# A six-layer decoder block on one core: the delta rule's inverse is taken within 64-token halves, the squares are added on GpSimd, its inputs are made in one block, and x is loaded and stored in pieces

## The chip, the core and the metric

The kernel is one program on one core of one Trainium2 chip. The metric is the device time in microseconds (us) of the whole program; lower is better. Three runs of the kernel before took 6059.12, 6057.47 and 6052.54 us, median 6057.47. The core's engines run side by side, each through its own list of instructions in order: PE (TensorE, matrix products), DVE (VectorE), ACT (ScalarE), POOL (GpSimd) and SP (SyncE, which here only starts DMAs). They meet at semaphores: an instruction adds to one when it is done, another waits until it has reached a number. An engine whose next instruction waits does nothing else.

## The reference, cut to what matters

x has 4 batches of 512 tokens of 512 features. Six layers follow each other: a selective scan, a quantised linear layer, a mixture of experts, the delta rule, a cross attention and a ternary feed-forward layer. The change touches the ends of the first and the last, and the delta rule, for which the reference steps through the tokens, for each of 16 heads of 128 features:

```python
q, k, v = (silu(causal conv(h @ W)) for each);  q = l2norm(q) * K ** -0.5;  k = l2norm(k)
g = -exp(A_log) * softplus(h @ Wfa @ Wfb + dt_bias);   beta = sigmoid(h @ Wb)
def step(S, (qt, kt, vt, gt, bt)):
    S = S * exp(gt)[..., None]
    vd = (vt - S^T kt) * bt
    S = S + kt[:, None] * vd[None, :]
    return S, S^T qt
o = o * rsqrt(mean(o * o) + eps) * o_norm_w * sigmoid(h @ Wga @ Wgb);   x = x + o @ Wo
```

Here h is the layer norm of x. Within a chunk of 128 tokens the vd of a token depends on those before it through a strictly lower triangular matrix L of 128 x 128, so the kernel needs (I + L)^-1 for each chunk, head and batch.

## The kernel before, in words

All of x stays in on-chip memory (`main_x_rows`, 16 tiles of 128 tokens). `load_constants` loads it by one DMA of 4 MB and waits for it, and each layer runs as a block of its own that starts when the one before has ended on every engine. `store_result` stores x by one DMA after the last block.

The delta rule has three blocks. `layer_norm` takes the statistics of all 16 tiles, normalises each, and turns it on PE into hT. `low_rank` multiplies hT by wfa, wga and wb for each batch (`low_f`, `low_g`, `low_b`), then takes the products with wb a second time with tokens on the partitions (`low_col`, 64 products of 16 columns), from which ACT makes root_beta. hT, fgT and beta go to HBM. `delta_heads` is the third.

`delta_heads` works on 64 units, one for each head and batch. A unit has four chunks of 128 tokens, side by side in tiles of 128 x 512. The program is written out by hand as a pipeline: a unit passes through four stages, `front`, `middle`, `late` and `back`, one iteration apart, and in each of the 27 numbered slots of an iteration every engine does what the four stages have there, the oldest unit first. So while unit n is in `front`, unit n-2 is in `late` and unit n-3 in `back`. Slot numbers alone set the order on each engine.

- `front`, slots 0 to 11: products with the projection weights (`delta_rule_proj`, `delta_rule_level` at the v projection), convolutions and norms on DVE and ACT.
- `front`, slots 12 to 24: seven levels, for halves of 1, 2, 4, ... 64 tokens. A level goes POOL `suffix` (L1816), DVE `prefix` (L2059), DVE `qk_second` (L2001), POOL `k_first` (L1807), PE `delta_rule_level` (L2182), and `take` on DVE, two copies under a mask into QT and L (L1990). PE has two banks for the levels, so the product of one level waits until `take` has read the one two before.
- `late`, slots 13 to 21: POOL has solved the 16-token blocks (`solve`), SP has carried them through HBM into X, and the list `steps` extends the inverse to 128 tokens. With W = X and R = L W, the full inverse is (I - R + R^2 - ...) applied to W: nine products, each four times 128 x 128, and each read from one of two banks by ACT (copies WT, R, R2, R4T) or DVE (copies RT, R2T; three sums into X).
- `back`, slots 0 to 12: for the four chunks in turn v - S^T k, its product with X, the new state, and o. Then ACT squares o, and two products with a matrix of ones (slot 13) add the squares of q and of o over the features. ACT takes logarithm and exponential (slot 20), DVE gates (slot 26).
- slot 23: the product of four kept units with w_o (L2265), and slot 26 its sum into x.

Each entry of `steps` is (slot, result, left, right, who reads it, ACT copies and DVE reads of the unit that PE waits for).

## Time and profile before

| | |
|---|---|
| runs of the whole program | 6059.12, 6057.47, 6052.54 us; median 6057.47 |
| the profiled execution, first to last instruction | 6055.8 us |
| PE, DVE, ACT, POOL busy | 81%, 65%, 47%, 35% of it |
| the pipeline of 64 units, from its first DMA on | 1744 to about 4800 us |
| the two blocks ahead of it (norm, low rank) | 1640 to 1744 us |
| load of x, store of x | issued at 0.94 us, at 6042.91 us |

The profiled execution's span is 1.7 us below the median of the runs. It is the same program in one execution, seen by the profiler. The profile gives busy time, what released each wait, and the order of time on each engine. The share of busy time does not tell what bounds a stage of a pipeline; for that the order of time is read engine by engine.

### The profile page before, as it was taken

How to read it: one execution, taken by the hardware profiler on the slowest of the kernel's cores; microseconds unless marked ns; L12 is line 12 of the kernel's file. 1: busy time of each engine (PE TensorE's matmuls, PEld its weight loads, DVE VectorE, ACT ScalarE, POOL GpSimd, SP SyncE). 2: the span in 40 equal slices, each digit the busy share in tenths (PEclk: the TensorE clock that was granted, in tenths of full speed). 3: DMA queues.
4: the chain of work that ended last, by engine and by line, in shares of the span. 5: the costliest groups of instructions: out<-in, count | busy, mean ns of one | idle time of the engine just before them, and what ended most of it. 6: DMA issues, size and time to landing. Idle time of an engine off the chain costs nothing. (4 is left out here: it accounts for less than half of the span.)

```text
span 6055.8 us, 82551 instructions
## 1 busy us (share of the span) xinstructions
PE 4922.0 (81%) x24879; PEld 3229.1 (53%) x24965; DVE 3961.2 (65%) x6588; ACT 2819.8 (47%) x5024; POOL 2139.0 (35%) x2663
## 2 busy tenths in 40 slices
PE   5788747999577889988998899899898665888856
PEld 3556534566345666666666666666666432444423
DVE  4677664222337877877777777787777244888756
ACT  5555352111124555555555555555555213777632
POOL 2455400110215545445455454454454044000100
PEclk8899868999778999999999999999999787999989
DMA  2111005244331111111111111111110044111110
GB/s 61 29 29 29 15 28 194 73 144 157 122 99 50 37 48 42 43 55 50 43 40 49 55 47 44 49 40 41 52 46 28 11 136 140 54 54 54 42 57 28
DMA packets 355563, 365.99 MB, mean 60 GB/s; under 512 B 100193, under 2 KB 253281, under 8 KB 353921
## 3 DMA queue, kind: packets, MB, share of 16 engines
q1 hardware_dynamic: 335472, 286.73, 15.9%
q0 software_dynamic: 19744, 74.99, 3.5%
q8 instruction: 176, 2.88, 0.2%
q14 instruction: 171, 1.39, 0.1%
HBM read 264.76 MB, written 96.86 MB: 60 GB/s over the span
## 5 line engine op out<-in xcount | busy, mean ns | idle before, releaser
L1816 POOL TENSOR_TENSOR delta_rule_suffix<-delta_rule_suffix,delta_rule_prefix 128x256 f32<-128x256 f32 x448 | 513.6, 1146 | 1141.5 <-ACT delta_rule_prefix L1911 715.6
L2158 PE MATMUL delta_rule_proj<-delta_rule_hT,delta_rule_w_qkv 128*128 128x512 f32 x1024 | 466.4, 599 | 0.0
L2182 PEld LDWEIGHTS delta_rule_level<-delta_rule_qk_second,delta_rule_k_first 128*128 128x128 f32 x3072 | 392.9, 196 | 101.3 <-issue 86.6
L2182 PE MATMUL delta_rule_level<-delta_rule_qk_second,delta_rule_k_first 128*128 128x128 f32 x3072 | 425.6, 283 | 24.9 <-DVE delta_rule_L_large L1990 9.6
L481 DVE TENSOR_TENSOR_SCAN scan_hs<-scan_decay,scan_inp 128x512 f32<-128x512 f32 x256 | 308.6, 1216 | 194.4 <-PE scan_inp L543 90.9
L315 POOL TENSOR_TENSOR scan_hc<-scan_hs,scan_c_rows 128x512 f32<-128x512 f32 x256 | 334.6, 1312 | 282.1 <-DVE scan_hs L481 266.1
L2001 DVE TENSOR_TENSOR delta_rule_qk_second<-delta_rule_qk,delta_rule_prefix 128x512 f32<-128x512 f32 x448 | 363.0, 810 | 47.4 <-issue 12.1
L2059 DVE TENSOR_TENSOR delta_rule_prefix<-delta_rule_prefix 128x256 f32<-128x256 f32 x448 | 287.1, 641 | 160.2 <-PE delta_rule_level L2170 121.1
L1807 POOL TENSOR_TENSOR delta_rule_k_first<-delta_rule_qk,delta_rule_suffix 128x256 f32<-128x256 f32 x384 | 304.5, 793 | 196.3 <-PE delta_rule_level L2170 155.9
L2006 DVE SCALAR_TENSOR_TENSOR delta_rule_qk<-delta_rule_proj,delta_rule_conv_w,delta_rule_qk 128x511 f32<-128x511 f32 (+2 forms) x384 | 287.5, 749 | 103.7 <-ACT delta_rule_qk L1890 76.8
L2666 DVE TENSOR_REDUCE attend_top<-attend_scores 128x1 f32<-128x512 f32 x512 | 327.6, 682 | 42.3 <-DMA scan_c_rows<-bc_dram 42.3
L2700 ACT ACTIVATE attend_probs<-attend_scores,attend_top 128x512 f32<-128x512 f32 x512 | 345.6, 685 | 5.0 <-DVE attend_top L2666 5.0
L543 PEld LDWEIGHTS scan_inp<-scan_b_diag,scan_duT 128*128 128x128 f32 x2048 | 277.1, 199 | 112.1 <-issue 107.4
L553 PE MATMUL scan_y_ps<-scan_hc,main_ident 128*128 128x512 f32 x512 | 273.7, 617 | 66.5 <-POOL scan_hc L315 66.2
L1945 ACT ACTIVATE delta_rule_R<-delta_rule_inv 128x512 f32<-128x512 f32 x192 | 114.6, 597 | 425.2 <-PE delta_rule_inv L2217 425.2
L2158 PEld LDWEIGHTS delta_rule_proj<-delta_rule_hT,delta_rule_w_qkv 128*128 128x128 f32 x1024 | 185.5, 191 | 227.2 <-issue 186.1
L2626 PEld LDWEIGHTS attend_turned<-main_ident,attend_probs 128*128 128x128 f32 x2048 | 229.6, 141 | 110.9 <-ACT attend_probsT L2713 93.9
L543 PE MATMUL scan_inp<-scan_b_diag,scan_duT 128*128 128x128 f32 x2048 | 281.7, 283 | 2.7 <-ACT scan_duT L395 2.7
L2618 PE MATMUL attend_scores<-attend_k_stack,attend_q_stack 128*128 128x512 bf16 x449 | 163.8, 390 | 146.9 <-ACT attend_probs L2700 97.8
L2626 PE MATMUL attend_turned<-main_ident,attend_probs 128*128 128x128 f32 x2048 | 274.9, 278 | 2.6 <-ACT attend_probs L2700 1.6
L2684 DVE COPY attend_probsT<-attend_turned 128x512 f32<-128x512 f32 x256 | 177.1, 692 | 123.7 <-PE attend_turned L2626 108.8
L2265 PE MATMUL delta_rule_seq<-delta_rule_w_o,delta_rule_o_kept 128*128 128x512 f32 x512 | 234.6, 602 | 10.7 <-DMA delta_rule_w_o<-in_kda_wo 5.7
(466 smaller groups left out, 11678.2 us busy)
## 6 DMA issues: line engine op xcount, KB each, us to landing
parts_dram<-qkv_parts POOLq DMA_DIRECT2D x64, 512.0 KB, 10.5
moe_w_d<-in_w_down SPq DMA_DIRECT2D x39, 512.0 KB, 4.3
scan_c_rows<-bc_dram SPq DMA_DIRECT2D x64, 256.0 KB, 3.7
delta_rule_w_qkv<-in_kda_wq SPq DMA_DIRECT2D x64, 256.0 KB
delta_rule_w_qkv<-in_kda_wk SPq DMA_DIRECT2D x64, 256.0 KB
delta_rule_w_qkv<-in_kda_wv SPq DMA_DIRECT2D x64, 256.0 KB
delta_rule_inv_beta<-beta_dram SPq DMA_DIRECT2D x64, 256.0 KB
delta_rule_w_o<-in_kda_wo SPq DMA_DIRECT2D x64, 256.0 KB, 4.7
```

The costliest lines, as they stand in the source:

```text
L315: pool.tensor_tensor(hc[:, u % RING, :], hs[:, u % RING, :], c_rows[:, n, :], ALU.mult).then_inc(weighed, 1)
L481: dve.tensor_tensor_scan(hs[:, u % RING, :], decay[:, u % RING, :], flat(inp_ps[u % INPUTS]), 0.0, ALU.mult, ALU.add).then_inc(scanned, 1)
L543: last = pe.matmul(inp_ps[u % INPUTS][:, c, :], duT[:, b % 2, c, k * P:(k + 1) * P], b_diag[:, n, c, :], start=True, stop=True)
L1807: pool.tensor_tensor(halves(k_first[:, i % 2, :], s, 0), halves(qk[p][:, 1, :], s, 0), first, ALU.mult).then_inc(k_ready, 1)
L1816: pool.tensor_tensor(first, first, whole_second, ALU.mult).then_inc(suffix_done, 1)
L2001: dve.tensor_tensor(qk_second[:, i % 2, :, :].rearrange("p j (n s) -> p j n s", s=s), qk[p][:].rearrange("p j (n two s) -> p j n two s", t ...
L2006: return dve.scalar_tensor_tensor(to[:, back_by:S], src[:, 0:S - back_by], conv_w[i][:, h, TAPS - 1 - back_by:TAPS - back_by], to[:, back_ ...
L2158: last = pe.matmul(to, w_qkv[p][:, i, k, :], hT[:, b % 2, k, :], start=(k == 0), stop=(k == DT - 1))
L2182: last = pe.matmul(level_ps[(i + 1) % 2][:, c, :], left, qk_second[:, i % 2, :, c * CHUNK // 2:(c + 1) * CHUNK // 2], start=True, stop=True)
L2626: last = pe.transpose(turned[i % 2][:, q, :], probs[:, j % 2, q, i * P:(i + 1) * P], g["ident"][:])
L2666: dve.tensor_reduce(top[:, j % 2, i:i + 1], scores[i][:], AX, ALU.max, negate=True).then_inc(max_done, 1)
L2700: act.activation(probs[:, j % 2, i, :], scores[i][:], ACT.Exp, bias=top[:, j % 2, i:i + 1], accum_out=head_sums[:, j % 2, i:i + 1]).then_i ...
```

## The change

1. x is loaded by four DMAs of 1 MB; nothing waits in `load_constants`, and the scan waits for batch b where it first reads it. x is stored tile by tile (256 KB) in the last block, as each tile is finished.
2. `layer_norm` and `low_rank` become one block, `delta_inputs`. The statistics are taken for the first 4 tiles, then for the other 12; a batch's low-rank products follow its turning; the four batches' products with wb (padded to 32 columns) go to four groups of 32 partitions of one bank; `low_col` is replaced by four transposes of exp(-b).
3. The inverse series stops within 64-token halves: R2 and R4T and the last sum go. The corner below the diagonal of the 128 x 128 inverse is made of 64 x 64 products: the first half's inverse turned (slot 21), times the corner of L (slot 23), times the second half's inverse (slot 25), and ACT copies each.
4. `take` of the last level copies its 64 x 64 corners without a mask, into QT and `L_top`.
5. POOL adds the squares of q to those of o in slot 17, and one product with ones in slot 19 takes the place of the two in slot 13.
6. SP returns the solved blocks of the first unit of a pair, waits for them and loads X, before it stores those of the second.

```diff
-                sp.dma_start(g["x"][:], g["x_dram"].rearrange("(t p) d -> p t d", p=P)).then_inc(x_loaded, 16)
-                sp.wait_ge(x_loaded, 16)
+                load_rows(sp, g, 0)
@@ scan, SP after dtproj
+                for b in range(1, B):
+                    load_rows(sp, g, b)
@@ scan, DVE, chores(b, 0)
+                        dve.wait_ge(g["x_loaded"][b], 16)
@@ last block, SP
+                    for t in range(NT):
+                        sp.wait_ge(out_added, t + 2)
+                        sp.dma_start(g["out_dram"][t * P:(t + 1) * P, :], g["x"][:, t, :]).then_inc(x_stored, 16)
+                    sp.wait_ge(x_stored, 16 * NT)
@@ delta_inputs, DVE
+                statistics(0)
+                invert(0)
+                for t in range(TPB):
+                    normalize(t)
+                statistics(1)
+                invert(1)
@@ delta_inputs, PE
+                def betas():
+                    for k in range(DT):
+                        for b in range(B):
+                            last = pe.matmul(b_ps[b * PAD:(b + 1) * PAD, :], wb[:, k, :], hT[:, k, b * S:(b + 1) * S],
+                                             start=(k == 0), stop=(k == DT - 1))
+                    last.then_inc(b_done, 1)
...
+                for t in range(TPB):
+                    turn(t)
+                pe.wait_ge(w_loaded, 32)
+                for b in range(1, B):
+                    for t in range(b * TPB, (b + 1) * TPB):
+                        turn(t)
+                    low_rank(b - 1)
+                betas()
+                low_rank(B - 1)
+                pe.wait_ge(b_exp, 1)
+                for i in range(TPB):
+                    last = pe.transpose(col_ps[:, i, :], beta[:, i * P:(i + 1) * P], g["ident"][:])
@@ delta_heads, slots and steps
-        SQUARE_SLOT, NORM_SLOT, LN_SLOT, EXP_SLOT, GATED_SLOT, OUT_SLOT, ADD_SLOT = 12, 13, 20, 20, 26, 23, 26
+        SQUARE_SLOT, SUM_SLOT, NORM_SLOT, LN_SLOT, EXP_SLOT, GATED_SLOT, OUT_SLOT, ADD_SLOT = 12, 17, 19, 20, 20, 26, 23, 26
...
                  (17, "W", "RT", "W", SUB, 2, 1),
-                 (17, "R2", "RT", "R", COPY_A, 2, 1),
-                 (17, "R2T", "R", "RT", COPY_V, 2, 2),
-                 (19, "W", "R2T", "W", ADD, 3, 3),
-                 (19, "R4T", "R2", "R2T", COPY_A, 3, 3),
-                 (21, "W", "R4T", "W", ADD, 4, 4)]
+                 (17, "R2T", "R", "RT", COPY_V, 2, 1),
+                 (19, "W", "R2T", "W", ADD, 2, 3),
+                 (21, TURN_FIRST, None, None, COPY_A, 2, 4),
+                 (23, CORNER_T, None, None, COPY_A, 3, 4),
+                 (25, CORNER, None, None, COPY_A, 4, 4)]
@@ SP, return_blocks
                     for p in range(2):
                         for c, to in enumerate(diagonal(g["solved_dram"][p])):
-                            sp.dma_start(to, block_rows(solved, p, c)).then_inc(solved_stored, 16)
-                    sp.wait_ge(solved_stored, 16 * 2 * CHUNKS * (m + 1))
-                    for p in range(2):
+                            sp.dma_start(to, block_rows(solved, p, c)).then_inc(solved_stored[p], 16)
+                        sp.wait_ge(solved_stored[p], 16 * CHUNKS * (m + 1))
@@ POOL, back
+                    if slot == SUM_SLOT:
+                        pool.wait_ge(o_squared, n + 1)
+                        pool.tensor_tensor(o_square[:], o_square[:], q_square[:, n % 4, :], ALU.add).then_inc(o_summed, 1)
@@ DVE, take
+                        if i == NL - 1:
+                            reach(dve, inv_done, NS * (n - 2) + 8)
+                            data = level_ps[(i + 1) % 2][:].rearrange("p c (j m) -> p c j m", j=2)
+                            dve.tensor_copy(QT[n % 3][FIRST, :, SECOND], data[FIRST, :, 0, :])
+                            dve.tensor_copy(L_top[p][:], data[FIRST, :, 1, :]).then_inc(level_read, 1)
+                            return
@@ PE, late
+                                if name == TURN_FIRST:
+                                    last = pe.transpose(inv_ps[i % 2][FIRST, c, FIRST], X[p][FIRST, c, FIRST], g["ident"][FIRST, FIRST])
+                                elif name == CORNER_T:
+                                    last = pe.matmul(inv_ps[i % 2][SECOND, c, FIRST], L_top[p][:, c, :], first_T[:, c, :], start=True, stop=True)
+                                elif name == CORNER:
+                                    last = pe.matmul(inv_ps[i % 2][FIRST, c, FIRST], corner_T[:, c, :], X[p][SECOND, c, SECOND],
+                                                     start=True, stop=True)
@@ PE, back
-                        pe.wait_ge(o_squared, n + 1)
+                        pe.wait_ge(o_summed, n + 1)
                         pe.wait_ge(state_done, (CHUNKS - 1) * (n + 1))
-                        pe.matmul(flat(seq_ps), g["ones"][:], q_square[:, n % 4, :], start=True, stop=False)
-                        pe.matmul(flat(seq_ps), g["ones"][:], o_square[:], start=False, stop=True).then_inc(o_norm_done, 1)
+                        pe.matmul(flat(seq_ps), g["ones"][:], o_square[:], start=True, stop=True).then_inc(o_norm_done, 1)
```

The first place is PE from slot 16 to the start of the next iteration, with buffer numbers (`inv0`, `level1`); a row is line, operation, what is written and read, and shape. Before:

```order
L2182 MATMUL delta_rule_level1<-delta_rule_qk_second,delta_rule_k_first 128x128 x4
L2217 MATMUL delta_rule_inv1<-delta_rule_X1,delta_rule_RT 128x128 x4
L2217 MATMUL delta_rule_inv0<-delta_rule_R,delta_rule_RT 128x128 x4
L2217 MATMUL delta_rule_inv1<-delta_rule_RT,delta_rule_R 128x128 x4
L2206 MATMUL delta_rule_proj1<-delta_rule_fgT,delta_rule_w_g 128x512
L2182 MATMUL delta_rule_level0<-delta_rule_qk_second,delta_rule_k_first 128x128 x4
L2217 MATMUL delta_rule_inv0<-delta_rule_X1,delta_rule_R2T 128x128 x4
L2217 MATMUL delta_rule_inv1<-delta_rule_R2T,delta_rule_R2 128x128 x4
L2182 MATMUL delta_rule_level1<-delta_rule_qk_second,delta_rule_k_first 128x128 x4
L2217 MATMUL delta_rule_inv0<-delta_rule_X1,delta_rule_R 128x128 x4
L2182 MATMUL delta_rule_level0<-delta_rule_qk_second,delta_rule_k_first 128x128 x4
L2265 MATMUL delta_rule_seq<-delta_rule_w_o,delta_rule_o_kept 128x512 x4
```

The same stretch of PE after the change, from R2T on:

```order
L2342 MATMUL delta_rule_inv0<-delta_rule_RT,delta_rule_R 128x128 x4
L2324 MATMUL delta_rule_proj1<-delta_rule_fgT,delta_rule_w_g 128x512
L2300 MATMUL delta_rule_level0<-delta_rule_qk_second,delta_rule_k_first 128x128 x4
L2377 MATMUL delta_rule_seq<-delta_rule_o_square,main_ones 128x512
L2342 MATMUL delta_rule_inv1<-delta_rule_X1,delta_rule_R2T 128x128 x4
L2300 MATMUL delta_rule_level1<-delta_rule_qk_second,delta_rule_k_first 128x128 x4
L2333 MATMUL delta_rule_inv0<-main_ident,delta_rule_X1 64x64 x4
L2300 MATMUL delta_rule_level0<-delta_rule_qk_second,delta_rule_k_first 128x128 x4
L2389 MATMUL delta_rule_seq<-delta_rule_w_o,delta_rule_o_kept 128x512 x4
L2335 MATMUL delta_rule_inv1<-delta_rule_RT,delta_rule_L_top1 64x64 x4
L2300 MATMUL delta_rule_level1<-delta_rule_qk_second,delta_rule_k_first 128x128 x4
L2337 MATMUL delta_rule_inv0<-delta_rule_X1,delta_rule_WT 64x64 x4
```

R2T goes to the other bank, the norm's product stands behind the fourth level, and two of the three small products stand behind the product with w_o. Between the first level and the next unit's projections there are three steps of four 128 x 128 products and one 128 x 512 product fewer, and three steps of four 64 x 64 ones more.

The second place is POOL in slots 14 to 18, before:

```order
L1807 TENSOR_TENSOR delta_rule_k_first<-delta_rule_qk,delta_rule_suffix 128x128x2
L1816 TENSOR_TENSOR delta_rule_suffix<-delta_rule_suffix,delta_rule_prefix 128x128x2
L1807 TENSOR_TENSOR delta_rule_k_first<-delta_rule_qk,delta_rule_suffix 128x64x4
L1816 TENSOR_TENSOR delta_rule_suffix<-delta_rule_suffix,delta_rule_prefix 128x64x4
L1807 TENSOR_TENSOR delta_rule_k_first<-delta_rule_qk,delta_rule_suffix 128x32x8
```

and after the change:

```order
L1915 TENSOR_TENSOR delta_rule_suffix<-delta_rule_suffix,delta_rule_prefix 128x128x2
L1906 TENSOR_TENSOR delta_rule_k_first<-delta_rule_qk,delta_rule_suffix 128x64x4
L1915 TENSOR_TENSOR delta_rule_suffix<-delta_rule_suffix,delta_rule_prefix 128x64x4
L1971 TENSOR_TENSOR delta_rule_o_square<-delta_rule_o_square,delta_rule_q_square 128x512
L1906 TENSOR_TENSOR delta_rule_k_first<-delta_rule_qk,delta_rule_suffix 128x32x8
```

The sum of the squares stands ahead of the fourth level's `k_first`. In both the slots of the levels are unchanged.

## Rows read from the trace of the kernel before

**Rows 1.** Order of time, first 30 us: start, length, engine, line, operation, idle before.

```profile
1.70 0.23 DVE L65 CAST main_ident<-main_ident 128x128 bf16<-128x128 f32 x1 [1.70 <-POOL main_ident L59]
...
19.81 2.46 DVE L438 BATCH_NORM_STATS2 scan_stats<-main_x_rows 128x6 f32<-128x512 f32 x4
```

**Rows 2.** DMA issues: destination, source, count, KB each, us to landing.

```profile
small_dram<-delta_rule_L_small SPq DMA_DIRECT2D x64, 256.0 KB, 2.0
...
main_x_rows<-in_x_dram SPq DMA_DIRECT2D x1, 4096.0 KB, 14.2
...
out_dram<-main_x_rows SPq DMA_DIRECT2D x1, 4096.0 KB, 12.5
...
fg_dram<-low_fgT SPq DMA_DIRECT2D x4, 512.0 KB, 3.1
```

**Rows 3.** Order of time, the last 16 us.

```profile
6041.26 0.75 DVE L2997 SCALAR_TENSOR_TENSOR main_x_rows<-ternary_ffn_out_ps,ternary_ffn_scales,main_x_rows 128x512 f32<-128x512 f32 x1 [6.43 <-PE ternary_ffn_out_ps L3027]
6042.91 0.39 SPq L74 DMA_DIRECT2D out_dram<-main_x_rows  x1
```

**Rows 4.** Order of time, norm and low rank, up to the pipeline's first DMA.

```profile
1640.19 9.59 DVE L101 BATCH_NORM_STATS2 norm_kda_stats<-main_x_rows  x16 [4.35 <-PEq L3119]
...
1652.33 1.01 DVE L113 TENSOR_SCALAR norm_kda_h<-main_x_rows,norm_kda_mean_var,norm_kda_rstd 128x512 f32 x2 [0.50 <-issue]
...
1687.39 3.60 PE L1440 MATMUL low_g<-kda_in_hT,low_wga 128*128 128x512 f32 x8
...
1715.66 24.35 PE L1445 MATMUL low_col<-low_wb,kda_in_hT 128*128 128x16 f32 x128
...
1744.24 0.41 SPq L1694 DMA_DIRECT2D delta_rule_conv_w<-in_conv_q_w  x1
```

**Rows 5.** Order of time, PE in the cross attention: products into four partition groups.

```profile
5121.13 1.06 PE L2638 MATMUL attend_out_ps<-attend_probsT,attend_v_head 128*32 128x512 f32 x8
```

**Rows 6.** A stretch: us, busy (count) of PE, PEld, DVE, ACT, POOL, granted clock, DMA.

```profile
1830.00:4650.00 2820.00, 2512.29 (x13286) 1771.07 (x13286) 2220.14 (x3676) 1497.64 (x2322) 1428.73 (x1853) 0.98 0.16 46
```

**Rows 7.** Order of time, PE, one unit's late slots, and the next unit's first product.

```profile
3023.04 1.13 PE L2217 MATMUL delta_rule_inv<-delta_rule_RT,delta_rule_R 128*128 128x128 f32 x8 [0.99 <-DVE delta_rule_X L2093]
...
3029.66 1.13 PE L2182 MATMUL delta_rule_level<-delta_rule_qk_second,delta_rule_k_first 128*128 128x128 f32 x8
3030.62 3.60 PE L2265 MATMUL delta_rule_seq<-delta_rule_w_o,delta_rule_o_kept 128*128 128x512 f32 x8
...
3034.95 0.60 PE L2192 MATMUL delta_rule_proj<-main_ident,delta_rule_k_square 128*128 128x128 f32 x4
...
3057.49 1.92 PE L2170 MATMUL delta_rule_level<-delta_rule_qk 128*128 128x128 f32 x8
```

**Rows 8.** Order of time, DVE, late slots of the same unit and of the next.

```profile
3015.99 0.99 DVE L2059 TENSOR_TENSOR delta_rule_prefix<-delta_rule_prefix 128x256 f32<-128x256 f32 x1
...
3019.95 0.42 DVE L2059 TENSOR_TENSOR delta_rule_prefix<-delta_rule_prefix 128x256 f32<-128x256 f32 x1
...
3022.16 0.73 DVE L2093 TENSOR_TENSOR delta_rule_X<-delta_rule_X,delta_rule_inv 128x512 f32<-128x512 f32 x1
3024.20 0.69 DVE L2091 COPY delta_rule_R2T<-delta_rule_inv 128x512 f32<-128x512 f32 x1 [1.31 <-PE delta_rule_inv L2217]
...
3029.09 0.43 DVE L1990 COPY_PREDICATED delta_rule_L_small<-delta_rule_level_mask,delta_rule_level 128x256 f32<-128x256 uint16 x1
```

**Rows 9.** Order of time, DVE, the next unit's copy of RT.

```profile
3065.85 0.69 DVE L2091 COPY delta_rule_RT<-delta_rule_inv 128x512 f32<-128x512 f32 x1 [0.78 <-PE delta_rule_inv L2217]
```

**Rows 10.** Order of time, POOL in the first of the two units.

```profile
3015.97 0.73 POOL L1807 TENSOR_TENSOR delta_rule_k_first<-delta_rule_qk,delta_rule_suffix 128x256 f32<-128x256 f32 x1
...
3017.12 1.23 POOL L1816 TENSOR_TENSOR delta_rule_suffix<-delta_rule_suffix,delta_rule_prefix 128x256 f32<-128x256 f32 x1 [0.43 <-DVE delta_rule_prefix L2059]
...
3032.13 1.27 POOL L1820 TENSOR_TENSOR delta_rule_k_square<-delta_rule_qk,delta_rule_suffix 128x512 f32<-128x512 f32 x1
```

**Rows 11.** What ended PEld's idle time before line 2215, 1830 to 4650: us, times.

```profile
  DMA delta_rule_X<-solved_dram: 17.7, 7
```

223 lines of the change are left out of this document (148 added, 75 removed).

## Prediction

> **What bounds the kernel now.** I read the ends of the program first, then the blocks ahead of the pipeline, then one unit of the pipeline engine by engine.
>
> At the start the whole 4 MB of x is waited for. It is issued at 0.94 us and lands 14.2 us later, at 15.1, while the other work of that block ends at 1.93 [rows 1, 2]. At the end the last sum into x is done at 42.01 (all times of that stretch are 6000 and more), the store starts at 42.91 and lands 12.5 us later, at 55.4 [rows 2, 3]. Both transfers stand alone on the path.
>
> The norm and low rank blocks take from 1640.19 to 1744.24, 104.0 us. The reader is to see that the engines work one after the other there: DVE takes all statistics for 9.6 us before anything is normalised, the products with wb run again as `low_col` for 24.35 us, and nothing of the pipeline starts before [rows 4].
>
> The pipeline is PE at first sight: 2512 of 2820 us busy, 89% [rows 6]. But the order of time of one unit shows two different halves. Of the level and inverse slots (about 3012.7 to 3035) the reader is to see that PE starts the level product at 3029.66 just 0.14 us after DVE ended the `take` that frees its bank (3029.09 + 0.43) [rows 7, 8]. DVE has been at work there with hardly a gap: its one long wait is 1.31 us for R2T, whose product PE itself held back 0.99 us because its bank still waited for DVE's sum into X [rows 7, 8]. So up to that level DVE's chain sets the pace, and PE's own work counts only behind it. From 3034.95 on the order is that of the projections and of the four chunks, which the change leaves as it is. The period is therefore read at 3034.95, the first product of the next iteration.
>
> **The start.** The block now ends at 1.93 plus the 0.5 us that lay between landing and the next block (15.1 to 15.6 before); everything behind moves by 15.1 - 1.93 = 13.2 us. x's first reader was at 19.81 and will be at about 6.6. The first 1 MB, issued at 0.94, must be there: between 2.0 us (256 KB) and 14.2 us (4 MB) [rows 2], by proportion 4.4, so it lands at 5.4. The other 3 MB are wanted much later. Parameter loads queue behind it and may lose 1 to 2 us. **Take 13; bounds 8 to 13.2.**
>
> **The end.** The last 256 KB are issued at about 42.1 and land 2.0 us later if like the 256 KB stores of the pipeline, at 44.1, and the 0.9 + 0.4 us of block end and program end remain: 45.4 for 55.8. **Take 10.4; bounds 0 (12.5 us whatever the size) and 10.4.** The other 15 stores lie beside the last layer's work.
>
> **The inputs.** Statistics of 4 tiles are 4 x 0.60 = 2.4 us (9.59 / 16); before, 2.5 us lay between the last statistic and the first normalised tile (1649.8 to 1652.33), for 4 tiles some 1.7. First tile at 1644.3, the four done at 1646.4 (0.5 each). Twelve more statistics take 7.2, and 2.3 for the root: 1655.9. The next four tiles are turned in 3 us: 1659. From there PE has work without a gap: four batches of two products of 3.60 are 28.8, eight tiles turned at 0.6, the time of four transposes [rows 7], 4.8, the wb products, and four transposes, 0.6 [rows 4]. The wb products now go to four partition groups. In the attention, eight such passes of 512 columns end within 1.06 us, where eight passes on the full width take 3.60 [rows 4, 5]: four times as fast. So 32 passes are 4 x 1.0 = 4.0, and 14.4 if the overlap failed. That gives 1697.2; PE's clock starts low, 2 us; then DVE's sum and two copies (2 us) and SP's store of fgT, 0.5 + 3.1 [rows 2]: about 1706 for 1744.2. **Take 38; bounds 27 and 41.** `low_col` is 24.35 of it, the rest is statistics and turning laid beside products.
>
> **One unit of the pipeline, normal clock.** Removed from PE: three steps of eight passes (0.9 each) and one product of 0.86; added: three steps of eight, eight and four short passes. On DVE one sum into X goes, behind the level that decides.
> - What the DVE chain gains. R2T goes to the other bank and no longer waits for the sum. DVE ends that sum at 3022.89 (3022.16 + 0.73), and would copy R2T at once instead of at 3024.20: 1.3 earlier.
> - What POOL's sum costs it. It starts when `suffix` of the third level ends, 3018.35, and takes 1.27 like the other 128 x 512 product [rows 10]; `k_first` follows, 3019.7 to 3020.5. DVE wants `prefix` at 3019.95. Beside a `k_first` (3015.97 + 0.73 = 3016.70) the same operation did not take 0.42 but 0.99 and ended at 3016.98, 0.28 behind it [rows 8, 10]. So it ends at 3020.8 instead of 3020.4: 0.4 later. Bounds: 0 and 1.3, the whole sum.
> - So `take` and the level product behind it come 0.9 earlier, 3028.8.
> - Behind it on PE: 5.29 us to 3034.95 as before, with the w_o product in it [rows 7], and now two short steps, CORNER_T and CORNER; the turning falls in a gap. No row shows a 64 x 64 product. A full pass is 0.11 of 128 columns, half the columns are 0.055, 0.45 a step; a 16-column pass is 0.19 at half clock (24.35 / 128, with full weight loads [rows 4]), 0.095 at full, 0.76 a step. I take 0.55, nearer to the columns, since here the weights are half as many too. Two steps: 1.1; bounds 0.9 and 1.8 (a full step each).
> - Sum: -0.9 + 1.1 = **+0.2 us a unit; bounds -0.4 and +0.9.** The moved norm product (slot 19) ends long before the logarithm is wanted for the w_o product; PE has room for it, since DVE decides.
>
> The Trainium skill, TensorEngine Tiling (Array Packing), section Tiling Modes, says that changing the tiling mode drains TensorE. This kernel would change it four times a unit on the path. By the attention's row, with its eight passes over in 1.06 us and its mode changed twice around them, that is next to nothing; by the page, a tail of some 0.2 us four times would make it 0.8 a unit more, 50 us: 6026, which is the second rival's case.
>
> **One unit with a clock dip.** Granted clock 0.98 over 2820 us means 2820 x 0.02 / 0.5 = 113 us at 1.2 GHz instead of 2.4 [rows 6]. At 3057.49, behind the chunks' products with their gaps, the eight passes take 1.92 instead of 1.13 and the next eight are slow too, some 3.3 us: about 34 dips, one in two units [rows 7]. In such a unit PE comes late, and DVE waits 0.78 for RT [rows 9]. The two norm products that lay ahead of it are gone, so this 0.78 is gained. Mean: +0.2 - 0.39 = -0.2 a unit, for 62 of the 64 units (the first and the last run partly alone) **-12 us; bounds -50 and +45.**
>
> **X.** PE waits seven times for X, 17.7 us in all [rows 11]. The first X of a pair is now asked for four stores earlier, 1.5 to 2 us each time, but PE also wants it earlier. **Take -8; bounds 0 and -14.**
>
> The wait of a unit's first chunk for the corner's copy has 4 us of projections ahead of it. SP's added wait stands before stores that nobody wants for one more unit. Both cost nothing.
>
> **Sum.** 6055.8 - 13 - 10.4 - 38 - 12 - 8 = 5974.4 in the profiled execution, which stands 1.7 below the median of the runs: **5976 us.**
>
> **Rivals.**
> - *PE sets the period after all.* Then a unit loses 3 x 0.9 + 0.86 - 0.45 - 2 x 0.55 = 2.0 us, 124 us instead of 12: 5864. For it: 89% busy, and that PE's removed work is large. Against it: the 0.14 us between `take` and the level product. 0.18, with half of it a mixture near 5920 (POOL's sum costs DVE nothing, short passes are cheap).
> - *The short products are dear* (drains, weight loads that nothing covers): 0.7 a unit more, 43 us: 6019. For it: no row has their price. Against it: the attention's row. 0.20.
> - *The clock, on the other side.* PE has gaps of about 1 us more in the level slots, where it waits for DVE. If the granted clock falls there too, in every unit, 3.3 us at 1.2 GHz lose 1.65 behind the deciding level, and the dip behind the chunks in every unit another 0.4: 2.05 x 62 = 127 us: 6103, slower. It decides from 82 / 62 = 1.3 us a unit. For it: dips follow stretches with gaps. Against it: PE stays over 80% busy in these slots, and I see dips only behind the chunks. 0.07. The Trainium skill, SBUF — State Buffer, section SBUF: two separate sides, has another way to lose: the port that VectorE and GpSimd share is locked by one for a whole instruction. By that rule POOL's sum could block DVE for 1.27 us a unit; the rows show 0.28 behind a shorter one, and the sum would be 54 us more, not enough alone.
> - *The change is not as told in the inputs* (products with wb not side by side): 10 us, inside the range.
>
> **How the numbers follow.** Forecast (DVE decides, the period stays within 0.5 us) 0.55, own range 5945 to 6010; PE's rival 0.18; dear products 0.20; clock 0.07. The measurement tells no change from one of 0.2%, 12 us. The three block terms give 61 us, and only the clock, or dear products at their worst together with a lost end, eats them: faster 0.90, same 0.03, slower 0.07. The range 5915 to 6035 leaves out the lower half of PE's rival (0.09) and most of the clock's.
>
> **What would show it.** The scan's first statistics at about 6.6 us; the last store landing within 3 us; `delta_inputs` 65 to 68 us long, with the 32 wb passes in about 4. In the pipeline: a period within 0.5 us of the one before; the level product ahead of the w_o product still within 0.2 us of the `take` that frees its bank; R2T's copy right behind the sum into X; the short steps 0.4 to 0.6 us each. A period shorter by over 1 us refutes the claim that DVE decides; one longer by as much says that the short products or the clock are dearer than taken.

## The result, and the profile after

The changed kernel takes 5991.01 us (median of 4 runs, 5984.97 to 5995.06) where the kernel before took 6055.66 in the runs beside it: a ratio of 0.9897, 95% interval 0.9884 to 0.991. The forecast was 5976, in a range of 5915 to 6035. The profiled execution spans 5993.5 us, 62.3 less than before. Between the places named by the rows ahead of the prediction, that difference is made up like this (gain in us, what was predicted in brackets):

| | | |
|---|---|---|
| up to the first statistics of the norm ahead of the pipeline | 1640.19 to 1627.17 | 13.0 (13) |
| from there to the pipeline's first DMA | 104.05 to 61.50 | 42.5 (38) |
| pipeline, from there to the next norm's statistics | 3071.16 to 3071.64 | -0.5 (20: 12 and 8 for X) |
| from there to the last sum into x | 1225.86 to 1229.44 | -3.6 (0) |
| from the last sum to the end | 14.54 to 3.75 | 10.8 (10.4) |

So the three block terms came, and the pipeline's 20 us did not. The 3.6 us lost behind it are spread over the blocks there, in which only the stores of x are new; 1.6 of them lie in the cross attention. That block has the same instructions throughout, and took 629.3 to 631.7 us in eleven of the fourteen profiled executions of this document and 638.5 to 638.6 in three. So a difference of this size is no sign of an effect. First the ends, in order of time (start, length, engine, line, operation, idle before and what ended it):

```profile
3.64 0.43 SPq L276 DMA_DIRECT2D scan_d_skip<-in_d_skip  x1
...
7.62 0.88 DVE L419 TENSOR_SCALAR scan_d_diag<-main_ident,scan_d_skip 128x128 f32<-128x128 f32 x4 [5.30 <-DMA scan_d_skip<-in_d_skip]
...
8.51 1.28 DVE L435 BATCH_NORM_STATS2 scan_stats<-main_x_rows 128x6 f32<-128x512 f32 x2
...
5989.75 0.75 DVE L3126 SCALAR_TENSOR_TENSOR main_x_rows<-ternary_ffn_out_ps,ternary_ffn_scales,main_x_rows 128x512 f32<-128x512 f32 x1 [6.17 <-PE ternary_ffn_out_ps L3156]
5990.52 0.33 SPq L3086 DMA_DIRECT2D out_dram<-main_x_rows  x1
```

The scan's first statistics start at 8.51 where they started at 19.81 [rows 1]; 6.6 was expected. The small load of d_skip, issued at 3.64, lands only at about 7.6. It takes 4.0 us where it took 1.7 in the kernel before: now the first 1 MB of x stands ahead of it in SP's queue. That is the 1 to 2 us that the prediction set aside for it. At the end 3.0 us are left behind the last sum, where there were 13.8 [rows 3].

The block of inputs, against [rows 4]:

```profile
1627.17 2.47 DVE L1454 BATCH_NORM_STATS2 kda_in_stats<-main_x_rows 128x6 f32<-128x512 f32 x4 [4.28 <-PEq L3249]
...
1632.72 7.21 DVE L1454 BATCH_NORM_STATS2 kda_in_stats<-main_x_rows 128x6 f32<-128x512 f32 x12
...
1671.80 3.64 PE L1550 MATMUL kda_in_b<-kda_in_hT,kda_in_wb 128*32 128x512 f32 x32
...
1682.34 0.60 PE L1565 MATMUL kda_in_col<-main_ident,kda_in_beta 128*128 128x128 f32 x4
...
1688.67 0.40 SPq L1794 DMA_DIRECT2D delta_rule_conv_w<-in_conv_q_w  x1
```

The 32 passes into four partition groups take 3.64 us, as the attention's row had it [rows 5]; four transposes replace the 24.35 us of `low_col`.

Now one unit of the pipeline at the normal clock, PE from the unit's first level to the next iteration's first product, against [rows 7]:

```profile
2997.51 1.06 PE L2288 MATMUL delta_rule_level<-delta_rule_qk 128*128 128x128 f32 x8
...
3001.23 1.13 PE L2300 MATMUL delta_rule_level<-delta_rule_qk_second,delta_rule_k_first 128*128 128x128 f32 x8 [1.33 <-DVE delta_rule_QT L2182]
...
3008.89 1.02 PE L2377 MATMUL delta_rule_seq<-delta_rule_o_square,main_ones 128*128 128x512 f32 x2
3009.76 1.05 PE L2342 MATMUL delta_rule_inv<-delta_rule_X,delta_rule_R2T 128*128 128x128 f32 x8
3011.01 1.13 PE L2300 MATMUL delta_rule_level<-delta_rule_qk_second,delta_rule_k_first 128*128 128x128 f32 x8 [0.20 <-DVE delta_rule_L_small L2108]
3012.07 0.41 PE L2333 MATMUL delta_rule_inv<-main_ident,delta_rule_X 64*64 64x64 f32 x4
3013.65 1.13 PE L2300 MATMUL delta_rule_level<-delta_rule_qk_second,delta_rule_k_first 128*128 128x128 f32 x8 [1.16 <-DVE delta_rule_L_small L2108]
3014.61 3.60 PE L2389 MATMUL delta_rule_seq<-delta_rule_w_o,delta_rule_o_kept 128*128 128x512 f32 x8
3018.14 0.68 PE L2335 MATMUL delta_rule_inv<-delta_rule_RT,delta_rule_L_top 64*64 64x64 f32 x8
3018.75 1.16 PE L2300 MATMUL delta_rule_level<-delta_rule_qk_second,delta_rule_k_first 128*128 128x128 f32 x8
3019.84 0.67 PE L2337 MATMUL delta_rule_inv<-delta_rule_X,delta_rule_WT 64*64 64x64 f32 x8
```

and DVE in the same unit, against [rows 8]:

```profile
3004.97 0.81 DVE L2177 TENSOR_TENSOR delta_rule_prefix<-delta_rule_prefix 128x256 f32<-128x256 f32 x1
...
3007.59 0.71 DVE L2211 TENSOR_TENSOR delta_rule_X<-delta_rule_X,delta_rule_inv 128x512 f32<-128x512 f32 x1
3008.22 0.67 DVE L2209 COPY delta_rule_R2T<-delta_rule_inv 128x512 f32<-128x512 f32 x1
...
3010.44 0.42 DVE L2108 COPY_PREDICATED delta_rule_L_small<-delta_rule_level_mask,delta_rule_level 128x256 f32<-128x256 uint16 x1
3010.85 0.69 DVE L2211 TENSOR_TENSOR delta_rule_X<-delta_rule_X,delta_rule_inv 128x512 f32<-128x512 f32 x1
...
3013.08 0.42 DVE L2108 COPY_PREDICATED delta_rule_L_small<-delta_rule_level_mask,delta_rule_level 128x256 f32<-128x256 uint16 x1
```

The reader is to see three things. The level product ahead of w_o (3013.65) starts 0.15 us behind the `take` (3013.50), as forecast, and R2T's copy stands right behind the sum into X. A short step occupies 0.61 us (3018.14 to 18.75) and the full step behind it 1.09 (3018.75 to 19.84) for 0.89 elsewhere. And DVE's last sum into X (3010.85) starts just as PE ends the product for it, 3009.76 and 0.89 and some 0.15 to be seen: 3010.8. The two engines arrive there together, which no row of before showed so plainly, and which the prediction did not weigh.

### The profile page after: what moved, and what is told of

Read it like the earlier page. It is cut to its first block and busy times, and to the rows that moved or that the text cites. A ratio compares the mean times of both kernels' runs of the same rounds, so it can differ in the third digit from the quotient of the medians.

```text
span 5993.5 us, 81416 instructions
## 1 busy us (share of the span) xinstructions
PE 4792.9 (80%) x24371; PEld 3098.5 (52%) x24457; DVE 3930.6 (66%) x6523; ACT 2807.4 (47%) x5085; POOL 2208.3 (37%) x2728
## 5 line engine op out<-in xcount | busy, mean ns | idle before, releaser
L2300 PE MATMUL delta_rule_level<-delta_rule_qk_second,delta_rule_k_first 128*128 128x128 f32 x3072 | 444.8, 289 | 174.4 <-DVE delta_rule_L_small L2108 105.3
L2177 DVE TENSOR_TENSOR delta_rule_prefix<-delta_rule_prefix 128x256 f32<-128x256 f32 x448 | 326.5, 729 | 171.1 <-PE delta_rule_level L2288 125.9
L2790 DVE TENSOR_REDUCE attend_top<-attend_scores 128x1 f32<-128x512 f32 x512 | 327.7, 682 | 42.5 <-DMA delta_rule_inv_beta<-beta_dram 42.5
L2730 POOL COPY attend_v_head<-xattn_v_tiles 128x64 f32 x128 | 24.5, 236 | 586.7 <-PE attend_out_ps L2762 586.3
```

The source lines that it names most:

```text
L2177: dve.tensor_tensor(halves(prefix[:], HALVES[i], 1), halves(prefix[:], HALVES[i], 1), whole_first, ALU.mult).then_inc(prefix_done, 1)
L2300: last = pe.matmul(level_ps[(i + 1) % 2][:, c, :], left, qk_second[:, i % 2, :, c * CHUNK // 2:(c + 1) * CHUNK // 2], start=True, stop=True)
L2790: dve.tensor_reduce(top[:, j % 2, i:i + 1], scores[i][:], AX, ALU.max, negate=True).then_inc(max_done, 1)
```

## The experiments

All changes are against the kernel after, where not said otherwise. "Period" is the distance between two units' first product of the next iteration (the place 3020.44 above) where the clock is normal; "slow" counts the units, of the 59 periods that follow the fifth start, that are 0.3 to 1.9 us longer. Some are longer still and not in that count: 3 before, 5 after, 11 in e_old_pipeline, 9 in e_squares_early, at most 6 elsewhere. Ratios are to the kernel before, with 95% intervals.

| | median us | ratio | period | slow |
|---|---|---|---|---|
| before | 6055.66 | 1 | 45.06 | 21 |
| after | 5991.01 | 0.9897 (0.9884 to 0.991) | 45.38 | 24 |
| e_old_pipeline | 6005.77 | 0.9914 (0.9901 to 0.9926) | 45.06 | 22 |
| e_sum_only | 6077.43 | 1.003 (1.002 to 1.004) | 46.08 | 38 |
| e_squares_early | 6018.82 | 0.9939 (0.9926 to 0.9953) | 45.12 | 26 |
| e_squares_pe | 6083.27 | 1.0051 (1.0038 to 1.0064) | 46.20 | 43 |
| e_copies_act | 5991.46 | 0.9891 (0.9876 to 0.9905) | 45.35 | 26 |
| e_norm_late | 5917.74 | 0.9771 (0.9759 to 0.9784) | 44.49 | 16 |
| e_corner_early | 5953.10 | 0.9824 (0.9808 to 0.984) | 44.64 | 24 |
| e_corner_double | 6083.68 | 1.0044 (1.0031 to 1.0056) | 46.31 | 50 |
| e_batch_late | 5984.51 | 0.9877 (0.9862 to 0.9891) | 45.38 | 26 |
| e_stores_first | 5998.78 | 0.9903 (0.9888 to 0.9918) | 45.38 | 21 |
| v_combined | 5871.24 | 0.9693 (0.968 to 0.9705) | 43.80 | 26 |
| v_squares_early | 5872.74 | 0.9692 (0.9679 to 0.9705) | 43.80 | 20 |

**e_old_pipeline**: the kernel before with parts 1 and 2 of the change alone.

> The kernel before with only the new ends (loads and stores of x in pieces) and the new block of inputs; the 64 units run as before. Theory 1 (by the traces: the pipeline's block lasted 3071.2 us before and 3071.6 after, so its change is worth nothing): 5990 us, as the kernel after within 6, ratio to before 0.989. Theory 2 (the pipeline gained its predicted 20 us and the three block terms gave less than the traces seem to say): 6011 us, ratio 0.993.

Measured 6005.8, between the two. Its profile runs the pipeline's old instructions at the old period of 45.06, and yet its pipeline, from the first DMA to the next norm's statistics, takes 3087.6 us where that of the kernel before took 3071.2. Of these 16 us, 11 lie in the 61 periods from the third start on (2811.8 for 2800.7): there are 22 slow units for 21, but 11 periods that are longer still for 3. So one profiled execution tells the pipeline's total no better than some 16 us. The pipeline's part of the change is worth about 15 us by the medians, 10 by the ratios (whose intervals overlap), 16 against this trace (3071.6 for 3087.6) and nothing against the trace of the kernel before. None of these is shown to be the right one. In the 61 periods alone the kernel after takes 2810.4 us, 1.4 less than this run and 9.7 more than the kernel before; the rest of each difference lies where the pipeline fills and empties.

**e_squares_pe**: back to two products, in slot 19, no sum on POOL.

```diff
...
-                        pe.wait_ge(o_summed, n + 1)
+                        pe.wait_ge(o_squared, n + 1)
...
-                        pe.matmul(flat(seq_ps), g["ones"][:], o_square[:], start=True, stop=True).then_inc(o_norm_done, 1)
+                        pe.matmul(flat(seq_ps), g["ones"][:], q_square[:, n % 4, :], start=True, stop=False)
+                        pe.matmul(flat(seq_ps), g["ones"][:], o_square[:], start=False, stop=True).then_inc(o_norm_done, 1)
```

> The kernel after, but the squares are not added on POOL: PE takes both products with the matrix of ones, in slot 19. Theory 1 (DVE's chain decides up to the level ahead of the w_o product, and POOL's sum holds up one prefix by 0.38 us a unit, while PE waits 1.17 us there and has room for 0.43 us more): period 45.0 for 45.38 us, 62 units, 24 us less: 5967 us, ratio 0.9855. Theory 2 (PE's work sets the pace): 0.43 us more a unit, 6018 us, ratio 0.994. Theory 3 (POOL's sum costs DVE nothing): 5991.

It went the other way: 92 us slower. Here my expectation also had a wrong price. One such product is 0.86 us, not 0.43 (in the unit above, 3008.89 to 3009.76). The period grew by 0.82, so nearly the whole product lay on the path, though PE had its wait of 1.17 us behind it. DVE in a unit of this run (a slow one; in the nine normal ones the wait is 1.18):

```profile
3037.37 0.69 DVE L2206 TENSOR_TENSOR delta_rule_X<-delta_rule_X,delta_rule_inv 128x512 f32<-128x512 f32 x1 [1.19 <-PE delta_rule_inv L2337]
```

DVE now stands still for 1.19 us ahead of the last sum into X, because PE is late with its product. PE's later wait for `take` is not room: it is the same lateness, handed on by DVE.

**e_copies_act**: RT and R2T copied by ACT.

```diff
-                 (15, "RT", "L_large", "WT", COPY_V, 1, 0),
+                 (15, "RT", "L_large", "WT", COPY_A, 1, 0),
...
-                 (17, "R2T", "R", "RT", COPY_V, 2, 1),
+                 (17, "R2T", "R", "RT", COPY_A, 3, 0),
...
```

The two counts at the end of the other entries follow from it.

> The kernel after, but RT and R2T are copied by ACT, not by DVE. Theory 1 (DVE's chain decides): DVE loses 0.69 + 0.68 us a unit; PE has 1.17 us of waiting to give, so the period falls by 1.0 to 1.2 us, 62 to 74 us in all: 5917 to 5929 us, ratio 0.977 to 0.979. Theory 2 (PE sets the pace, its wait of 1.17 us is given back elsewhere): 5991. Theory 3 (ACT does R and RT one after the other and comes late for PE): 5991 to 6020.

Nothing changed, 5991.5. Theory 1, which was the prediction's, falls. PE and then DVE in a unit of this run (a slow one; in the normal ones the medians of the two waits are 1.59 and 0.89):

```profile
2962.83 1.05 PE L2342 MATMUL delta_rule_inv<-delta_rule_X,delta_rule_R2T 128*128 128x128 f32 x8
...
2966.73 1.13 PE L2300 MATMUL delta_rule_level<-delta_rule_qk_second,delta_rule_k_first 128*128 128x128 f32 x8 [1.59 <-DVE delta_rule_L_small L2108]
```

```profile
2963.93 0.69 DVE L2211 TENSOR_TENSOR delta_rule_X<-delta_rule_X,delta_rule_inv 128x512 f32<-128x512 f32 x1 [0.90 <-PE delta_rule_inv L2342]
```

The time taken from DVE came back as 0.90 us of waiting for PE's product, and PE's wait for the `take` grew from 1.17 to 1.59 us.

**e_norm_late**: the copies on ACT as in e_copies_act, and the norm product behind that product.

```diff
-        SQUARE_SLOT, SUM_SLOT, NORM_SLOT, LN_SLOT, EXP_SLOT, GATED_SLOT, OUT_SLOT, ADD_SLOT = 12, 17, 19, 20, 20, 26, 23, 26
+        SQUARE_SLOT, SUM_SLOT, NORM_SLOT, LN_SLOT, EXP_SLOT, GATED_SLOT, OUT_SLOT, ADD_SLOT = 12, 17, 20, 20, 22, 26, 23, 26
```

> RT and R2T are copied by ACT, and the norm product stands in slot 20, behind the product for the last sum into X (slot 19), the exponential in slot 22. With the copies alone on ACT the time did not change: DVE then waited 0.90 us for that product, behind the level and the norm product on PE. Theory 1 (PE's list up to that product and then DVE's 2.9 us of sum, prefix, second halves and take set the pace together): the product comes 0.43 us earlier and so does the deciding level: 27 us less, 5964 us, ratio 0.985. Theory 2 (DVE alone decides): as with the copies alone, 5991. Theory 3 (PE decides everywhere, an order of its list changes nothing): 5991 too, and DVE's wait for the product then shrinks without the level product coming earlier.

Theory 1 holds, with the right price: the period fell by 0.86 us, one product with ones, against the copies alone. DVE's last sum follows its `take` without a wait:

```profile
2890.28 0.42 DVE L2108 COPY_PREDICATED delta_rule_L_small<-delta_rule_level_mask,delta_rule_level 128x256 f32<-128x256 uint16 x1
2890.72 0.69 DVE L2211 TENSOR_TENSOR delta_rule_X<-delta_rule_X,delta_rule_inv 128x512 f32<-128x512 f32 x1
```

The time fell by 74 us, which is more than 62 times 0.86 (53). Of the other 21 us the two profiles put 9 in the slow units, which went from 26 to 16, 3 in the periods that are longer still, and 7 in the cross attention, where e_copies_act is one of the three executions with 638.6 us and this one took 631.7.

**e_corner_early**: CORNER_T in slot 22, CORNER in slot 24.

```diff
-                 (23, CORNER_T, None, None, COPY_A, 3, 4),
-                 (25, CORNER, None, None, COPY_A, 4, 4)]
+                 (22, CORNER_T, None, None, COPY_A, 3, 4),
+                 (24, CORNER, None, None, COPY_A, 4, 4)]
```

> The kernel after, but CORNER_T stands in slot 22 and CORNER in slot 24 (23 and 25). Theory 1 (a short step costs only where PE is on the path): CORNER_T falls into PE's wait of 1.17 us for DVE; what was 0.61 us, and 0.19 us on the level behind it, is gone: 0.6 to 0.8 us a unit, 37 to 50 us: 5941 to 5954 us, ratio 0.981 to 0.983. Theory 2 (ACT's copy of the turned half comes too late, and the level behind waits in its turn): 0 to 0.4 us a unit more, 5991 to 6016. Theory 3 (a short step's price is a drain at each change of its shape, paid wherever it stands): 0.2 to 0.3 us a unit less, 5975.

As theory 1 had it: period 0.74 us less, 38 us in all. (62 times 0.74 is 46, and its profiled pipeline is 47 us shorter; its cross attention took 7.6 us more, see the result.) PE:

```profile
2898.51 0.41 PE L2333 MATMUL delta_rule_inv<-main_ident,delta_rule_X 64*64 64x64 f32 x4
2899.48 0.67 PE L2335 MATMUL delta_rule_inv<-delta_rule_RT,delta_rule_L_top 64*64 64x64 f32 x8 [0.56 <-ACT delta_rule_RT L2051]
2900.09 1.15 PE L2300 MATMUL delta_rule_level<-delta_rule_qk_second,delta_rule_k_first 128*128 128x128 f32 x8
```

The short step fills what was PE's wait, and the level starts with no wait at all. So a short step was free in the gap, and cost 0.61 + 0.2 us behind the deciding level.

**e_corner_double**: every product of CORNER_T and CORNER issued twice.

```diff
+                            if name in (CORNER_T, CORNER):
+                                for c in range(CHUNKS):
...
                             for c in range(CHUNKS):
```

> The kernel after, but each of the products of CORNER_T and of CORNER is issued twice (eight 64 x 64 products a step for four, into the same place): 16 more short passes a unit on the path. Theory 1 (a short step's 0.61 us is the price of its eight passes, 0.076 us each): 1.2 us a unit more, 62 units, 75 us: 6066 us, ratio 1.002. Theory 2 (a drain at each change of shape makes up most of it and the passes themselves take 0.03 us or less, by their 64 columns): 0.5 us a unit or less, up to 30 us: 6021 us, ratio 0.994 or less.

The period grew by 0.93 us for 16 passes, 0.058 each, between the theories. PE in a slow unit of this run:

```profile
3002.52 0.68 PE L2334 MATMUL delta_rule_inv<-delta_rule_RT,delta_rule_L_top 64*64 64x64 f32 x8
3003.04 0.63 PE L2342 MATMUL delta_rule_inv<-delta_rule_RT,delta_rule_L_top 64*64 64x64 f32 x8
3003.59 1.16 PE L2300 MATMUL delta_rule_level<-delta_rule_qk_second,delta_rule_k_first 128*128 128x128 f32 x8
3004.68 0.68 PE L2336 MATMUL delta_rule_inv<-delta_rule_X,delta_rule_WT 64*64 64x64 f32 x8
```

Eight passes are 0.46 us; the other 0.15 of a step's 0.61, and 0.2 more on the full step behind it, do not depend on their number. The median is 92.7 us up, where 62 times 0.93 is 58. The rest is slow units, 50 of 59: by the profiles they cost 46 us more than in the kernel after, and some 10 come back elsewhere.

**e_squares_early**: both products in slot 13, no sum on POOL (the diff shows the slots alone). **e_sum_only**: e_old_pipeline with the sum on POOL and one product in slot 19.

```diff
-        SQUARE_SLOT, SUM_SLOT, NORM_SLOT, LN_SLOT, EXP_SLOT, GATED_SLOT, OUT_SLOT, ADD_SLOT = 12, 17, 19, 20, 20, 26, 23, 26
+        SQUARE_SLOT, SUM_SLOT, NORM_SLOT, LN_SLOT, EXP_SLOT, GATED_SLOT, OUT_SLOT, ADD_SLOT = 12, 17, 13, 20, 20, 26, 23, 26
```

> The kernel after, but the squares are added on PE as before the change: both products with ones in slot 13, none in slot 19, and no sum on POOL. The earlier runs priced a product with ones at 0.86 us (two halves of 0.43). Theory 1 (PE's list up to the product for the last sum into X sets the pace with DVE behind it): in slot 13 the two products take 1.72 us, of which 1.3 fall into PE's wait for DVE's copy of the diagonal blocks; slot 19 gives 0.86 back and DVE loses the collision with POOL: 0.4 to 0.5 us a unit less, 5960 to 5966 us, ratio 0.985. Theory 2 (adding on POOL is worth its PE time, 0.86 us a unit): 53 us more, 6044 us.

> The kernel before with the new ends and inputs (6005.8 us in its own runs), and of the pipeline's change only the squares' sum on POOL (slot 17) with one product in slot 19; the inverse series is the old one. Theory 1 (as for the run above, seen from the other side): slot 13 gives back 0.4 us (1.72 less the wait that opens there), slot 19 costs 0.86 on the path: 0.4 to 0.5 us a unit more, 6031 to 6037 us, ratio 0.996. Theory 2 (a product less on PE is a gain wherever it stands): 0.86 us a unit less, 5953 us.

The signs of the normal period are theory 1's (-0.26 us in the first, +1.02 in the second, expected 0.4 to 0.5 each way), but the sizes and the first run's time, 28 us above the kernel after, are not. The normal units first. Two rows of PE and two of DVE in e_sum_only:

```profile
3278.82 1.13 PE L2282 MATMUL delta_rule_level<-delta_rule_qk_second,delta_rule_k_first 128*128 128x128 f32 x8 [0.23 <-DVE delta_rule_L_small L2090]
3285.61 1.02 PE L2352 MATMUL delta_rule_seq<-delta_rule_o_square,main_ones 128*128 128x512 f32 x2
```

```profile
3279.41 0.82 DVE L2159 TENSOR_TENSOR delta_rule_prefix<-delta_rule_prefix 128x256 f32<-128x256 f32 x1
...
3287.57 0.69 DVE L2193 TENSOR_TENSOR delta_rule_X<-delta_rule_X,delta_rule_inv 128x512 f32<-128x512 f32 x1 [0.84 <-PE delta_rule_inv L2317]
```

The product of the fourth level (3278.82) starts 29.25 us behind the start of its iteration, exactly as in e_old_pipeline, since it waits for `take` there. So slot 13 gives nothing back in a normal unit. POOL's sum then costs DVE a net 0.17 us, and the product in slot 19 its whole 0.86: 1.03 for the 1.02 measured. Seen from the other side, in e_squares_early PE starts its product for the last sum 0.88 us earlier in the iteration than in the kernel after, and the period falls only by what DVE gains without POOL's sum. PE waits for it at the next level:

```profile
2974.76 1.13 PE L2295 MATMUL delta_rule_level<-delta_rule_qk_second,delta_rule_k_first 128*128 128x128 f32 x8 [0.84 <-DVE delta_rule_L_small L2103]
```

What I had left out besides is what slot 13 does in a slow unit. There PE loses 1.6 us in the first two levels; in the kernel after, its wait for DVE's copy of the diagonal blocks shrinks from 1.33 to 0.79 us (median of the 24; 0.51 in the unit shown, which is 2.5 us longer and not among the 24) and takes part of that up:

```profile
3042.88 1.87 PE L2288 MATMUL delta_rule_level<-delta_rule_qk 128*128 128x128 f32 x8
3044.54 1.92 PE L2300 MATMUL delta_rule_level<-delta_rule_qk_second,delta_rule_qk 128*128 128x128 f32 x8
...
3047.41 1.13 PE L2300 MATMUL delta_rule_level<-delta_rule_qk_second,delta_rule_k_first 128*128 128x128 f32 x8 [0.51 <-DVE delta_rule_QT L2182]
```

With the products in slot 13 nothing is left to shrink, and a slow unit is 1.63 us longer (46.75), as before the change (1.61), where it is 1.06 in the kernel after. That cancels the 0.26. The 61 periods take 10.7 us more than after, and seven of the nine periods that are longer still have a second stretch at 1.2 GHz, in the level ahead of w_o and in w_o, behind PE's wait of 1.09 us:

```profile
3024.07 2.04 PE L2295 MATMUL delta_rule_level<-delta_rule_qk_second,delta_rule_k_first 128*128 128x128 f32 x8 [1.09 <-DVE delta_rule_L_small L2103]
3025.91 4.23 PE L2385 MATMUL delta_rule_seq<-delta_rule_w_o,delta_rule_o_kept 128*128 128x512 f32 x8
```

The profiled execution is 21.9 us longer than that of the kernel after. 11 of these are in the pipeline, 8 in the cross attention (638.6 for 630.9), 4 ahead of the pipeline, where nothing was edited. The other 6 of the 28 us are in no trace.

**e_batch_late**: the next batch's 1.5 MB are issued at the end of their iteration.

```diff
-                    if i % HEADS == 4 and i // HEADS + 1 < B:
-                        load_batch(i // HEADS + 1)
...
                     if i < N:
                         send_blocks(i)
+                    if i % HEADS == 4 and i // HEADS + 1 < B:
+                        load_batch(i // HEADS + 1)
```

> The kernel after, but the loads of the next batch's hT and fgT (1.5 MB) are issued at the end of their iteration, behind the iteration's return of the solved blocks and its sending of blocks, not ahead of them. Theory 1 (PE's four waits for X, 21.3 us, are the pairs whose blocks and X queue behind these loads; the order of the eight stores matters little): three of the four waits go, 12 to 16 us less: 5975 to 5979 us, ratio 0.987, and in the profile X is waited for once or not at all. Theory 2 (the waits come from the stores and loads of the pair itself): 5991, four waits as before.

**e_stores_first**: eight stores, then both X, as before the change.

```diff
                             sp.dma_start(to, block_rows(solved, p, c)).then_inc(solved_stored[p], 16)
-                        sp.wait_ge(solved_stored[p], 16 * CHUNKS * (m + 1))
+                    for p in range(2):
+                        sp.wait_ge(solved_stored[p], 16 * CHUNKS * (m + 1))
+                    for p in range(2):
```

> The kernel after, but all eight stores of a pair's solved blocks are issued and landed before the first X is asked for, as before the change. Theory 1 (PE waits for X only at the start and where the next batch's loads stand ahead in the queue; four stores more or less do not matter): 5991 within 5, the same four waits. Theory 2 (the prediction's term of 8 us, by the order of the stores): 5999 us, ratio 0.991.

PEld's waits for X over 1690 to 4815, in us, times, longest: the kernel after, then e_batch_late, then (us and times alone) e_stores_first. In the kernel before it was 22.0 us in 8.

```profile
PEld delta_rule_inv L2340 <- DMA delta_rule_X<-solved_dram: 21.3, 4, 6.2
```

```profile
PEld delta_rule_inv L2340 <- DMA delta_rule_X<-solved_dram: 6.1, 4, 4.7
```

```profile
  DMA delta_rule_X<-solved_dram: 34.9, 18
```

Without the new order of stores the new series waits 18 times, 13.6 us more in all. With it, it waits as long as before the change, in four places: the three iterations that load a batch, and the last pair, where the pipeline empties. Moving those loads takes 15 us of waiting away, and the 61 periods are 9.9 us shorter; the median fell by 6.5 us (12 by the ratios), with intervals that overlap. The median of e_stores_first is 7.8 us higher, as the prediction's 8, but only 4 by the ratios, and the 61 periods of its profile are 5.6 us shorter than those of the kernel after. That the order of stores is worth time is not shown; that it takes waiting away is.

**v_combined**: copies on ACT, norm product in slot 20, exponential in 22, the turning in 20, CORNER_T in 21, CORNER in 24, batch loads late. **v_squares_early**: the same with both products in slot 13 and no sum on POOL.

> A version of its own: copies RT and R2T on ACT, norm product in slot 20, exponential in slot 22, the turning in slot 20, CORNER_T in slot 21, CORNER in slot 24, and the batch's loads at the end of their iteration. Theory 1 (the two lists set the pace together; a short step costs only on the path): the early corner is worth 38 us, the norm product behind the last sum's some 0.4 to 0.5 us a unit, 25 to 30 us, the late batch loads 12: 5910 to 5916 us, ratio 0.976. Theory 2 (with the corner moved, DVE's chain of takes decides alone): 5953 - 12 = 5941, ratio 0.981.

> The combined version (5871 us) with both products with ones in slot 13 and no sum on POOL. Theory 1 (the same 0.4 to 0.5 us a unit, from PE's slot 20 and from DVE's prefix and second halves, which stand beside POOL's sum): 25 to 30 us less, 5841 to 5846 us, ratio 0.965. Theory 2 (at a period of 43.8 us DVE's levels alone decide, and only its collision with POOL's sum goes): 0.2 us a unit or less, 5859 to 5871.

5871 us, 3.1% below the kernel before and 2.0% below the kernel after, some 40 below what was expected; period 43.80. The second version is the same within 2 us, with the same period to 0.01. That is theory 2's number, but not its reason: what DVE saves without POOL's sum it loses by waiting for PE's product, 0.73 us, since PE's list up to it has kept its length:

```profile
3040.54 0.69 DVE L2206 TENSOR_TENSOR delta_rule_X<-delta_rule_X,delta_rule_inv 128x512 f32<-128x512 f32 x1 [0.73 <-PE delta_rule_inv L2337]
```

In v_combined PE and DVE again arrive together at the level ahead of w_o:

```profile
2915.61 0.67 PE L2335 MATMUL delta_rule_inv<-delta_rule_RT,delta_rule_L_top 64*64 64x64 f32 x8
2916.22 1.16 PE L2300 MATMUL delta_rule_level<-delta_rule_qk_second,delta_rule_k_first 128*128 128x128 f32 x8
```

```profile
2915.62 0.42 DVE L2108 COPY_PREDICATED delta_rule_L_small<-delta_rule_level_mask,delta_rule_level 128x256 f32<-128x256 uint16 x1
```

## Why the prediction was right, and where it was wrong

- **The start, the end, the inputs** (13, 10.4, 38): 11.3 at the first statistics and 13.0 by the norm, 10.8, 42.5. Right in mechanism; the inputs are past the upper bound of 41. Of the 4.3 us 1.2 were a slip (the terms given add up to 1704.8, not to 1706), 1.6 the low clock of the first product, set at 2 and measured at 0.4 (4.04 us for 3.60), the rest shorter steps on PE.
- **"DVE's chain sets the pace, and PE's own work counts only behind it."** This step failed, though its sum came near. PE's list up to the product for the last sum into X and DVE's list up to the same place are equally long; behind it comes DVE's sum, prefix, second halves and `take`. Shown by four runs: 1.37 us less on DVE gives nothing, 0.86 more on PE costs 0.82, both eased give 0.86, and 0.88 less on PE with only DVE's collision with POOL gone gives 0.26 (e_squares_early). PE's list eased by itself, with nothing else changed, was not run. The 0.14 us between `take` and the level [rows 7, 8] told who came last there, not what DVE itself had waited on.
- **-0.9 up to the deciding level.** Measured 1.24 us, from the unit's first level product (3012.28 to 3029.66 before, 2997.51 to 3013.65 after). POOL's sum held DVE's prefix as forecast: 0.81 where it had been 0.42. But only half of these 0.4 us reached the path, since RT's copy just ahead no longer waits 0.18 for PE. And R2T's copy came 1.4 earlier, not 1.3.
- **+1.1 for the two short steps.** Measured 1.50 (5.29 to 6.79): a term that was too small. The passes are near the estimate; what was missed is a fixed part, 0.57 us a unit (1.50 less 16 times 0.058). The Trainium skill, TensorEngine Tiling (Array Packing), section Tiling Modes, says that a change of mode drains TensorE. The trace agrees in that a fixed part is there; the prediction's estimate by that rule was 0.8 us a unit, and the fixed part is seven tenths of it. That it is a drain, and not weight loads that nothing covers, no run tells apart. My reading of the attention's row, that it is next to nothing, was wrong.
- **The period** was to grow by 0.2 us and grew by 0.32: 7 us. That it is so near is luck: the gain up to the deciding level was 0.34 larger than forecast, the cost behind it 0.4.
- **0.78 us gained in every second unit.** A slow unit's excess fell by 0.55, from 1.61 to 1.06, and there were 24 of 59, before 21. By the periods that is 34 to 25.5 us: 9 gained for 24. The count of 34, taken from a clock of two digits, was too high.
- **X, 8 us.** Waits of 22.0 us became 21.3. The earlier request takes 13.6 us of waiting away against the same series without it, but PE's earlier demand took that back, and three of the four waits stand behind a batch's loads, which I had not looked for.
- **The rivals.** PE alone did not set the period (5864). The dear short products came about half way: 0.4 of the 0.7 us a unit. The clock fell behind the chunks, as before. It fell in the level slots too, around the product with w_o, as the third rival had it, but in 3 of 59 units and not in all (none before the change); in e_squares_early it was 8.

The sum for the profiled execution missed by 19 us (5974.4 for 5993.5), the forecast of the median by 15: 20 expected in the pipeline and not seen in the trace, 3.6 lost behind it without a cause I know, 4.9 more gained ahead of it and at the end. The forecast came into its range by the three block terms, 66 of the 62 us gained; the pipeline's part, which most of the reasoning was about, was worth nothing to 16 us, by which trace one compares.

## What to carry to other kernels

When an engine starts right behind another's release, follow the releaser back too: a wait is only room if the engine that ends it was not itself waiting for the one that waits. Two lists that meet at several places must be eased together: easing DVE's alone gave nothing, easing PE's by 0.88 us gave the 0.26 that DVE had to give, easing both gave 0.86 us a unit. Put small fixed-cost steps into the gap that the meeting leaves, not behind it, and keep large loads out of a queue ahead of a transfer that the path is about to want.
